# Mixture of experts run batch by batch, with the neighbouring stages of the other batch interleaved into its steps

## The reference

```
x = x + full_attention(layernorm(x))      # A: 16 heads of width 8, 1024 keys
x = x + moe(layernorm(x))                 # M1
x = x + banded_attention(layernorm(x))    # B: 16 heads, each query sees 32 keys
x = x + moe(layernorm(x))                 # M2, the same weights as M1
```

## Time and profile before

| stage | from, us | to, us |
|---|---|---|
| setup, projections and attention A | 0 | 453.0 |
| output projection A | 453.0 | 470.0 |
| norm and routing M1 | 470.0 | 508.5 |
| experts M1 | 508.5 | 780.5 |
| norm and projections B | 780.5 | 817.0 |
| attention B | 817.0 | 957.0 |
| output projection B | 957.0 | 974.5 |
| norm and routing M2 | 974.5 | 1015.8 |
| experts M2 and the output's stores | 1015.8 | 1289.2 |

### The profile page before, as it was taken

The page is one execution under the profiler, slowest core; times in us unless marked ns, Lnnn a source line. Parts: engine busy times, 40 slices in busy tenths (PEclk is TensorE's granted clock), DMA queues, the critical chain, the costliest instruction groups (busy, mean ns, idle before and its releaser), DMA issues. The chain is left out here.

```text
span 1289.2 us, 21879 instructions
## 1 busy us (share of the span) xinstructions
PE 1087.0 (84%) x6296; PEld 437.9 (34%) x6296; DVE 1031.3 (80%) x1765; ACT 720.8 (56%) x1103; POOL 400.7 (31%) x316
## 2 busy tenths in 40 slices
PE   4599999899998462999999995598975499999997
PEld 2112222222221051344444443233344244444443
DVE  6798999899999778788888886455537788888886
ACT  3207777677778522566666666045543356666665
POOL 1000000000000302676777770000001267777675
PEclk9658999899999776999999998589986699999999
DMA  2800000000002810767776651312100177766663
GB/s 66 249 4 26 26 27 1 27 26 21 6 2 93 278 32 3 162 161 166 161 162 158 155 117 47 102 52 58 45 2 20 44 177 165 159 156 155 162 161 95
DMA packets 53388, 120.14 MB, mean 93 GB/s; under 512 B 10296, under 2 KB 36792, under 8 KB 45128
## 3 DMA queue, kind: packets, MB, share of 16 engines
q1 hardware_dynamic: 53320, 119.28, 37.2%
HBM read 103.94 MB, written 14.91 MB: 92 GB/s over the span
## 5 line engine op out<-in xcount | busy, mean ns | idle before, releaser
L476 DVE TENSOR_REDUCE Aatt_mx<-Aatt_sc 128x1 f32<-128x512 f32 x512 | 317.4, 683 | 25.5 <-PE Aatt_sc L352 25.0
L436 ACT ACTIVATE Aatt_prob<-Aatt_st 128x1024 f32<-128x1024 f32 x256 | 247.3, 1022 | 76.5 <-PE Aatt_st L361 75.0
L1392 POOL TENSOR_TENSOR M1ex_low<-M1ex_hid,M1ex_high 128x512 f16<-128x512 f32 x132 | 180.8, 1387 | 95.0 <-ACT M1ex_high L1324 92.1
L1392 POOL TENSOR_TENSOR M2ex_low<-M2ex_hid,M2ex_high 128x512 f16<-128x512 f32 x132 | 179.6, 1378 | 94.5 <-ACT M2ex_high L1324 93.2
L352 PE MATMUL Aatt_sc<-ks,qs 48*128 48x512 bf16 x512 | 176.9, 432 | 27.3 <-DVE Aatt_mx L476 5.8
L372 PE MATMUL Aatt_pv<-Aatt_prob,vg 128*32 128x512 f32 x1024 | 143.4, 633 | 0.8 <-ACT Aatt_prob L436 0.6
L1363 DVE TENSOR_TENSOR M1ex_hid<-M1ex_act_up,M1ex_cb 128x512 f32<-128x512 f32 x132 | 138.4, 1049 | 4.9 <-DMA M1ex_cb<-comb 4.9
L1363 DVE TENSOR_TENSOR M2ex_hid<-M2ex_act_up,M2ex_cb 128x512 f32<-128x512 f32 x132 | 139.0, 1053 | 4.0 <-DMA M2ex_cb<-comb 4.0
L1354 DVE SCALAR_TENSOR_TENSOR M1ex_act_up<-M1ex_up,unscale,M1ex_sil 128x512 f32<-128x512 f32 x132 | 98.4, 746 | 37.0 <-ACT M1ex_sil L1319 34.6
L1319 ACT ACTIVATE M1ex_sil<-M1ex_gate,unscale 128x512 f32<-128x512 f32 x132 | 90.7, 687 | 64.9 <-PE M1ex_gate L1272 61.1
L1354 DVE SCALAR_TENSOR_TENSOR M2ex_act_up<-M2ex_up,unscale,M2ex_sil 128x512 f32<-128x512 f32 x132 | 98.4, 746 | 35.4 <-ACT M2ex_sil L1319 31.2
(11 more groups left out here) (271 smaller groups left out, 1774.8 us busy)
## 6 DMA issues: line engine op xcount, KB each, us to landing
M1ex_cb<-comb SPq DMA_DIRECT2D x64, 512.0 KB, 6.5
M2ex_cb<-comb SPq DMA_DIRECT2D x64, 512.0 KB, 6.5
M_wt<-wsplit SPq DMA_DIRECT2D x66, 192.0 KB
wsplit<-split_cut SPq DMA_DIRECT2D x9, 704.0 KB, 7.0
split_raw<-in_wg_dram SPq DMA_DIRECT2D x6, 704.0 KB, 5.1
stack<-Aqkv_part SPq DMA_DIRECT2D x16, 192.0 KB, 3.2
qs<-stack SPq DMA_DIRECT2D x32, 96.0 KB
ks<-stack SPq DMA_DIRECT2D x32, 96.0 KB
```

The costliest lines, as they stand in the source:

```text
L436: act.activation(prob[e % 4][:, :, :].rearrange("p a c -> p (a c)"), st[pr][:, :, :].rearrange("p a c -> p (a c)"), ACT.Exp, scale=SCALE). ...
L476: dve.tensor_reduce(mx[k][:, m, part // 2:part // 2 + 1], sc_bank(k, i)[:, :], AX.X, ALU.max).then_inc(red_done, 1)
L1392: pool.tensor_tensor(low[i % 3][:, :], hid[i % 3][:, :], high[i % 3][:, :], ALU.subtract).then_inc(low_ready, 1)
```

## The change

Each MoE layer is done batch by batch. The 132 steps stay 132, but the first 66 are batch 0 (33 pairs by 2 chunks) and the last 66 batch 1, so that the matrices of each pair are loaded twice. The other stages are cut in the same way:

- `first_batch` does, alone, the output projection, norm and routing of batch 0, and stores its weights.
- In `experts`, one slot of output projection, norm and routing of batch 1 stands beside each of the first 42 steps. Each engine's program is a Python generator, and `next(beside)` puts the next piece into a step. On TensorE the piece stands between gate/up of step q and down of step q-3, on ACT behind `silu` and `high`, on DVE behind `act_up` and `hid`, on POOL behind `low`.
- In M1, from step 74 on, norm and projections of layer B for batch 0 stand beside the steps in the same way (16 slots). `qkv_of_batch` then does batch 1 alone, ahead of attention B.
- PSUM is divided anew: three banks in a ring for gate and up (`gate` of step q takes over the bank of `up` of step q-2, `up` of step q that of `gate` of step q-1), two for `acc`, three for the work beside. `times_up` writes its result in place into the `up` bank, and `times_weight` reads it there.
- Rings are six buffers for matrices and five of half the width for `cb`. The steps are written out instead of looped. The stores of `comb` and `stack` are issued on ACT's queue instead of SP's (in `first_batch`, `experts` and `qkv_of_batch`).
- Attention A and its projections stay as they were.

```diff
+def out_tensor(pe, env, o, bank, b):
+    def turn(i):
+        for h in range(2):
+            t = 2 * i + h
+            if i:
+                pe.wait_ge(o.att_ready, t - 1)
+            for g in range(G):
+                mm = pe.transpose(bank[h][:, g * P:(g + 1) * P], env.u[:, G * b + g, t * P:(t + 1) * P], env.ident[:, :])
+            mm.then_inc(o.ut_done, 1)
+    def turn_back(i):
+        pe.wait_ge(o.att_ready, 2 * i + 2)
+        if i:
+            pe.wait_ge(o.x_ready, i)
...
+    for i in range(ROUNDS_OUT):
+        if i:
+            project(i - 1)
+        turn(i)
+        yield
+        yield
+        turn_back(i)
+        yield
+    project(ROUNDS_OUT - 1)
+    yield
...
+def norm_of_batch_scalar(act, env, n, bank):
+    yield
+    yield
+    yield
+    act.wait_ge(n.var_ready, 1)
+    act.activation(n.sd[:, :], n.ve[:, :], ACT.Sqrt).then_inc(n.sd_ready, 1)
...
+def route_scalar(act, env, n, q, bank, b):
+    for c in range(2):
...
+        act.copy(env.xh[:, cs], n.xnT[:, c * CH:(c + 1) * CH]).then_inc(env.xh_ready[b], 1)
+        yield
+    act.wait_ge(q.lg_done, 2)
+    act.activation(q.sc[:, :, :], bank[2][:, :].rearrange("p (t e) -> p t e", t=TB), ACT.Sigmoid).then_inc(q.sig_ready, 1)
+    for _ in range(ROUTE_SLOTS - 4):
+        yield
+    for c in range(2):
+        act.wait_ge(q.comb_turned, c + 1)
+        act.copy(q.combT[:, c * CH:(c + 1) * CH], bank[c][0:ROWS, :]).then_inc(q.comb_copied, 1)
+        act.wait_ge(q.comb_copied, c + 1)
+        act.dma_start(env.comb_rows[:, b * S + c * CH:b * S + (c + 1) * CH],
+                      q.combT[:, c * CH:(c + 1) * CH]).then_inc(env.comb_stored[b], 16)
+        yield
...
+def qkv_scalar(act, env, v, bank, b):
...
+    def store(i):
+        act.wait_ge(v.low_ready, 2 * i + 2)
+        act.wait_ge(v.mid_ready, 2 * i + 2)
+        for g in range(G):
+            act.dma_start(env.stack[i, b * G + g].rearrange("s r t -> r s t"),
+                          v.part[32 * g:32 * g + 32, i, :, :]).then_inc(env.stored[b], 16)
...
+    HB = 2 * PAIRS
+    QN = B * HB
+    LAG = 3
+    UPDATE = HB + LAG + 2
+    AFTER = UPDATE + 3
...
+        gate = lambda q: ring[2 * q % 3]
+        up = lambda q: ring[(2 * q + 1) % 3]
...
+                if q >= 2:
+                    pe.wait_ge(hid_ready, q - 1)
+                pe.matmul(gate(q)[:, :], wt[k][:, 0, :], env.xh[:, cs], start=True, stop=False)
+                pe.matmul(gate(q)[:, :], wt[k][:, 0, :], env.xl[:, cs], start=False, stop=False)
+                pe.matmul(gate(q)[:, :], wt[k][:, 1, :], env.xh[:, cs], start=False, stop=True).then_inc(g_done, 1)
+                if q >= 1:
+                    pe.wait_ge(sil_ready, q)
...
+            for q in range(QN):
+                gate_up(q)
+                if q < HB:
+                    next(beside, None)
+                if q in (UPDATE, UPDATE + 1):
+                    back(0, q - UPDATE)
+                if q >= AFTER:
+                    next(behind, None)
+                if q >= LAG:
+                    down(q - LAG)
...
-                act.wait_ge(down_done, q + 1)
-                act.wait_ge(hid_ready, ONE + q + 1)
+            def high_part(q):
+                if q >= 3:
+                    act.wait_ge(down_done, q - 2)
+                act.wait_ge(hid_ready, q + 1)
...
-                dve.scalar_tensor_tensor(act_up[i % 3][:, :], up[i % 2][:, :], env.unscale[:, 1:2], sil[i % 2][:, :],
+                dve.scalar_tensor_tensor(up(q)[:, :], up(q)[:, :], env.unscale[:, 1:2], sil[q % 2][:, :],
...
-                dve.tensor_tensor(hid[i % 3][:, :], act_up[i % 3][:, :], cb[k][:, c * CH:(c + 1) * CH],
+                dve.tensor_tensor(hid[q % 3][:, :], up(q)[:, :], cb[k][:, c * CH:(c + 1) * CH],
...
+            for q in range(QN):
+                times_up(q)
+                times_weight(q)
+                if q < HB:
+                    next(beside, None)
```

More of the change, by code:

```diff
@@ new lines, in qkv_scalar, with high, middle @@
+def qkv_scalar(act, env, v, bank, b):
+    def high(k):
+        i, c = QK[k]
+        act.wait_ge(v.mm_done, k + 1)
+        act.activation(v.part[:, i, HIGH[i], c * CH:(c + 1) * CH], bank[(k + 2) % 3][:, :], ACT.Identity,
+                       bias=env.bqk[:, i:i + 1]).then_inc(v.high_ready, 1)
+    def middle(k):
+        i, c = QK[k]
+        act.wait_ge(v.rest_ready, k + 1)
+        act.copy(v.part[:, i, MID[i], c * CH:(c + 1) * CH], v.rest[:, k % 3, :]).then_inc(v.mid_ready, 1)
+    def store(i):
[4 more added lines that the diff above has]
+                          v.part[32 * g:32 * g + 32, i, :, :]).then_inc(env.stored[b], 16)
+    high(0)
+    yield
+    for k in range(1, 4):
+        middle(k - 1)
+        high(k)
+        if k == 3:
+            store(0)
+        yield
+    middle(3)
+    yield
+    yield
+    store(1)
+    yield
@@ L1083, in _ @@
         def _(pe):
[L1084 to L1090 removed]
+            rest_of(out_tensor(pe, env, o, bank, 0))
+            rest_of(norm_of_batch_tensor(pe, env, n, bank))
+            rest_of(route_tensor(pe, env, n, q, bank))
@@ L1313, in _, with before, after @@
                 mm.then_inc(back_done, 1)
+            def before():
+                yield from out_tensor(pe, env, o, bank, 1)
+                yield from norm_of_batch_tensor(pe, env, n1, bank)
+                yield from route_tensor(pe, env, n1, q1, bank)
+            def after():
+                if not last:
+                    yield from norm_of_batch_tensor(pe, env, n2, bank)
+                    yield from qkv_tensor(pe, env, n2, v2, bank)
+            beside, behind = before(), after()
@@ new lines, in after @@
+            def after():
+                if not last:
+                    dve.wait_ge(x_ready, 2)
+                    yield from norm_of_batch_vector(dve, env, n2, 0)
+                    yield from qkv_vector(dve, env, v2, bank, 0)
+            dve.tensor_copy(cb[0][:, :], env.unscale[:, 3:4].to_broadcast([P, S])).then_inc(cb_filled, 1)
+            dve.wait_ge(cb_filled, 1)
+            beside, behind = before(), after()
+            for q in range(QN):
+                times_up(q)
+                times_weight(q)
+                if q < HB:
+                    next(beside, None)
+                if q in (UPDATE, UPDATE + 1):
+                    update(0, q - UPDATE)
+                if q >= AFTER:
+                    next(behind, None)
@@ L1398, in moe @@
+            beside = before()
+            for q in range(QN):
+                pool.wait_ge(high_ready, q + 1)
+                if q >= 3:
+                    pool.wait_ge(down_done, q - 2)
+                pool.tensor_tensor(low[q % 3][:, :], hid[q % 3][:, :], high[q % 3][:, :], ALU.subtract).then_inc(low_ready, 1)
+                if q < HB:
+                    next(beside, None)
+def moe(nc, env, tag, last=False):
     with ExitStack() as ctx:
```

825 lines of the change are left out of this document (490 added, 335 removed).

## The result

The changed kernel takes 1299.64 us in the median of nine runs (1293.69 to 1306.37) where the kernel before takes 1291.98 (nine runs on the same chip): ratio 1.0059, with a 95% interval of 1.0031 to 1.0087. It is slower by 0.6%, or 7.7 us; 1296 was forecast, +4.5 us on the profiled execution. The profiled execution of the changed kernel took 1293.69 us (span 1291.9), 2.6 us more than that of before.

The account below looks back on a forecast made before the run. TensorE was taken to bound experts, DVE or chains of waits the other stages. M1 +24.5, M2 +14.7, heads -9.7 and -12.7, projections of B -12.3 gave +4.5 on 1291.06: forecast 1296 us, range 1277 to 1314.

Parts of the forecast that it names:

- What bounds: Whole kernel: stages in a row, TensorE full in experts at 1.94 us a plain step, DVE or chains of waits elsewhere.
- The rival that transfers cannot keep up: Experts: transfers staying at 165 GB/s would make half a layer take 141 us instead of 128; 1309 us, chance 0.05.
- Heads: End of attention to experts, with batch 0 alone: 45.8 us for M1 (gain 9.7), 46.1 for M2 (gain 12.7).
- Projections of B: Norm and projections of batch 1 alone, ahead of attention B: 24.2 us instead of 36.5, gain 12.3.
- Experts without work beside: Bare expert steps with start, tail and end: 265.2 us for M1 (272.0 before), 268.3 for M2 (273.4 before).
- `hid` near 690 ns without a spread: DVE in experts: `hid`, with an operand now in PSUM, priced at 0.69 us, with bounds of 0.68 and 1.05.
- The rival that `hid` stays at 1.05: Experts: each DVE-bound slot costs 0.36 us more, +19 in all, giving 1315 us; chance 0.09.
- Beside batch 0: First half of experts, both layers: batch 1's work costs 19.8 us a layer, TensorE 9.8 plus DVE and ACT stalls 10.0.
- the stalls of routing: Routing slots beside batch 0: long DVE slots, the sigmoid's two loads and POOL's product stall TensorE 6.8 us a layer.
- Beside batch 1: Second half of experts M1: layer B's norm, products and stores for batch 0 cost 11.5 us.
- The rival of absorption: Work beside in experts is absorbed: 1283 us at half the stalls, 1271 with none; chance 0.34.
- The rival of a dearer table switch: ACT beside the steps: a further 1.4 us behind each of ten loads, +14, giving 1310 us; chance 0.03.

Follow-up runs that it names:

- Number 5: Changed kernel with batch 0's output projection tile by tile over more PSUM banks (three, two, two): 1281.16 us, ratio 0.9925 to the kernel before.
- number 3: Changed kernel with batch 1's output projection, norm and routing alone in a second block, both layers: 1350.70 us, ratio 1.0424 to the kernel before.
- number 4: Changed kernel with layer B's norm and projections for batch 0 alone in a block of their own: 1311.47 us, ratio 1.0131 to the kernel before.
- number 2: Changed kernel with `act_up` in an SBUF buffer again, so `hid` reads two SBUF operands: 1339.23 us, ratio 1.034 to the kernel before.
- number 1: Changed kernel with Identity in place of root and sigmoid beside the experts' steps, so no table changes there: 1289.46 us, ratio 0.9974 to the kernel before.
- Number 6: Changed kernel with the work beside cut finer, 15 norm slots and 32 routing slots: 1285.95 us, ratio 0.9970 to the kernel before.
- number 10: The changed kernel itself measured and profiled once more, with no edit: 1300.41 us, ratio 1.0057 to the kernel before.

## Why the prediction came out right

- **What bounds.** TensorE, in plain steps: 1.94 us in both layers, as forecast, at 183 to 192 GB/s of transfers. The rival that transfers cannot keep up is out.
- **Heads.** 46.1 and 45.7 us for 45.8 and 46.1, a sum that is partly luck. In M1 the output projection took 17.0, not 14.9: its rounds stand end to end at 3.57 us (3.6 forecast), but the first, at the lower clock, took 4.85. The 1.4 for the layer's end lies ahead of the head's first mark, and the choice with the turning and storing of `comb` took 18.8 for 19.6; that made up for it. Number 5 shows that the rounds were worth 14.6 us. The norm took 6.9 for 6.8. Casts, table and sigmoid were sized 3.1 and took 3.3, but not as a sum on ACT: TensorE's logits set that time.
- **Projections of B.** 22.6 for 24.2, a gain of 14.1 for 12.3. ACT issues four stores in 2.2 us rather than 2.6, and the first four beside its own activations.
- **Experts without work beside.** 297.8 less the 22.2 of number 3 and the 10.1 of number 4 is 265.5 for M1 (265.2 forecast), 289.8 less 22.0 is 267.8 for M2 (268.3).
- **`hid` near 690 ns without a spread.** 691 to 693. With two operands in SBUF it spreads to 1696 (number 2), so where the operand lies is the cause. The Trainium skill (SBUF — State Buffer, "Who interferes with whom") has a DVE instruction with two SBUF inputs contend with a GpSimd instruction that reads SBUF. The traces agree in both directions. The rival that `hid` stays at 1.05 was priced 1315 and would have been 1339: its +19 counted only slots with work in them, not the plain steps.
- **Beside batch 0.** 22.2 and 22.0 for 19.8. The term that was too small is the stalls of routing, put at 6.8 beside TensorE's 2.7; the 20 slots lasted 11.8 us more than plain steps, not 9.5. What was not in the sum is in step 38: small instructions that wait for the whole of `low`. The loads were priced too low as well: the root's pair 1.8 for 2.1, the sigmoid's 1.0 for 1.64 (number 1). Norm was 4.6 for 4.1, output projection 5.9 (its 6.9 less 1.0 for the start) for 6.2.
- **Beside batch 1.** 10.1 for 11.5. Silu was 1.9 us late behind the stores, as forecast, but TensorE lost 0.34 there, not 1.2: its next gate was not due yet.
- **The rival of absorption.** It needed the stalls under 18.3 us (the forecast had 25.4, though its own terms give 25.2); they were 28.4 (12.4, 12.2 and 3.8 beyond TensorE's own work). Number 6 took about 14 us of them away by cutting the slots up. So DVE's total was not the limit, the order in time was; in number 6 DVE is busy 44.5 of 55.0 us beside routing. That rival's mechanism was possible, in another kernel than this one.
- **The rival of a dearer table switch.** Out: 2.1 and 1.64 us for a pair of loads (number 1), no more than they last.

The forecast of +4.5 against +6.8 in the trace is two errors of the same sign (+1.5 and +1.9 in the experts) less one of the other (-1.8 in the projections), with +0.4 and +0.2 in the heads. That they nearly cancel is luck; the mechanism (full stages, stalls beside, rounds end to end) is what the runs bear out.

## What to carry to other kernels

Work put beside a full engine is worth its saving only if each piece fits the free time of every engine in its step: measure plain steps, take the free time of the second engine and the slack to the next due operand, and cut pieces to that. A stage halved in work is not halved in time when it has fewer banks; look at whether its rounds overlap. And an operand placed in PSUM instead of SBUF can be worth more than the instruction's own length, because it keeps two engines apart.

## What was not expected of the hardware

- A small VectorE instruction from SBUF can last as long as the GpSimd instruction beside it: `quota` 0.94 us against 0.17, a tile of `xn` 1.28 against 0.34. `quota` ends at 591.56, where `low` ends at 591.53, and the tile of `xn`, which started 0.03 us ahead of a `low`, at 680.54, where that `low` ends at 680.45. The Trainium skill (SBUF — State Buffer, "Who interferes with whom") has a `tensor_scalar` in a two-port mode and a GpSimd instruction lock each other out for a whole instruction; these ends agree, though no row shows the mode.
- A single wait of 2.07 us in TensorE was followed by 3.3 us at the lower clock in both layers of the changed kernel, and not in numbers 1 and 5, whose code there is the same. TensorE lost 1.7 us by it and the kernel nothing, since DVE set the pace of those steps.
- The same stage with the same code had a granted clock of 0.80, 0.63 or 0.50 over its first 17 us in three executions, and took 17.0, 18.65 or 21.0 us (number 10).
- DMA issues on ScalarE's queue run beside its activations: four took 2.2 us, and the activation among them kept its 0.68.
